# Transposing and splitting the cross-attention's context inside the self-attention stage, one batch per step

## The reference

```
x = x + self_attention(norm(x))
k = (ctx @ Wk); v = (ctx @ Wv)                  # ctx: (32, 375, 256)
x = x + softmax(norm(x) @ Wq · k / sqrt(128)) @ v @ Wo
x = x + expert(argmax(norm(x) @ wg), norm(x)) * gate
```

## Time and profile before

| | us |
|---|---|
| median of 3 runs | 2617.39 (2616.61 to 2623.79) |
| the profiled execution, its own time | 2618.37 |
| its span, first to last instruction | 2616.6 |
| PE (TensorE) busy | 2451.6 |
| PEld (its weight loads) busy | 2231.8 |
| DVE (VectorE) busy | 1759.5 |
| ACT (ScalarE) busy | 1262.5 |
| POOL (GpSimd) busy | 1050.3 |

### The profile page before, as it was taken

The page is one execution under the profiler, slowest core; times in us unless marked ns, Lnnn a source line. Parts: engine busy times, 40 slices in busy tenths (PEclk is TensorE's granted clock), DMA queues, the critical chain, the costliest instruction groups (busy, mean ns, idle before and its releaser), DMA issues. The chain is left out here.

```text
span 2616.6 us, 45419 instructions
## 1 busy us (share of the span) xinstructions
PE 2451.6 (94%) x14878; PEld 2231.8 (85%) x14878; DVE 1759.5 (67%) x4953; ACT 1262.5 (48%) x3220; POOL 1050.3 (40%) x1475
## 2 busy tenths in 40 slices
PE   5999999689999999999999989999999999999598
PEld 5888888578998989899898979999999999898476
DVE  6878887375756666565757576666757576666676
ACT  4555554364545445454545454554545454545311
POOL 3433443043434334343434343444435343434354
PEclk9999999799999999999999999999999999999799
DMA  7221223331211212122222121111111111110543
GB/s 243 73 68 57 69 67 100 110 108 53 76 64 54 68 62 77 50 72 64 72 88 62 60 69 49 58 57 38 56 56 59 48 46 56 50 35 29 185 153 122
DMA packets 98213, 195.09 MB, mean 75 GB/s; under 512 B 19696, under 2 KB 50128, under 8 KB 97728
## 3 DMA queue, kind: packets, MB, share of 16 engines
q1 hardware_dynamic: 92192, 163.68, 19.7%
q0 software_dynamic: 5600, 18.41, 2.1%
q10 hardware_dynamic: 224, 10.49, 1.2%
HBM read 127.21 MB, written 75.81 MB: 78 GB/s over the span
## 5 line engine op out<-in xcount | busy, mean ns | idle before, releaser
L1242 POOL TENSOR_SCALAR x_probs<-x_probs,x_inv 112x376 f32<-112x376 f32 x512 | 634.5, 1250 | 190.3 <-DVE x_inv L1450 190.3
L1302 ACT ACTIVATE x_probs<-x_probs,x_bias 112x376 f32<-112x376 f32 x512 | 308.4, 603 | 423.1 <-POOL x_bias L1236 423.0
L1236 POOL TENSOR_SCALAR x_bias<-x_top 112x1 f32<-112x1 f32 x512 | 124.0, 242 | 957.3 <-DVE x_top L1422 957.0
L1570 PE MATMUL x_ps_f<-x_xT,x_wq 128*128 128x448 f32 x1536 | 344.4, 374 | 12.3 <-DVE x_ctxT L1400 5.8
L1584 PE MATMUL x_ps_r<-x_wo,x_oT 128*128 128x512 f32 x1344 | 343.8, 392 | 1.4 <-DVE x_wo L1355 1.4
L1521 PEld LDWEIGHTS x_ps_o<-x_pT,x_v 128*128 128x128 f32 (+1 forms) x2304 | 294.9, 191 | 30.4 <-DVE x_pT L1429 12.7
L1570 PEld LDWEIGHTS x_ps_f<-x_xT,x_wq 128*128 128x128 f32 x1536 | 283.0, 190 | 44.0 <-DVE x_v L1400 8.8
L1521 PE MATMUL x_ps_s<-x_kT,x_qT 128*112 128x376 f32 x1536 | 312.0, 338 | 3.0 <-DVE x_top L1422 3.0
L1521 PE MATMUL x_ps_f<-x_ctxT,x_wk 128*128 128x376 f32 x1536 | 308.3, 337 | 2.5 <-DVE x_kT L1400 1.3
L1521 PE MATMUL x_ps_f<-x_wv,x_ctxT 128*128 128x512 f32 (+1 forms) x1152 | 304.6, 402 | 4.8 <-DVE x_kT L1400 4.8
L1521 PE MATMUL x_ps_o<-x_pT,x_v 128*128 128x224 f32 (+1 forms) x2304 | 298.9, 274 | 8.4 <-DVE x_pT L1429 8.4
(11 more groups left out here) (205 smaller groups left out, 3825.7 us busy)
## 6 DMA issues: line engine op xcount, KB each, us to landing
x_ctxs<-x_ctxT SPq DMA_DIRECT2D x32, 752.0 KB, 4.1
x_ctxT<-x_ctxs SPq DMA_DIRECT2D x32, 752.0 KB, 4.3
x_xT<-h2T SPq DMA_DIRECT2D x16, 896.0 KB
room<-in_ctx_dram SPq DMA_DIRECT2D x32, 256.0 KB
m_wn<-in_L_ffn_W_dram SPq DMA_DIRECT2D x32, 256.0 KB
x2r<-sums SPq DMA_DIRECT2D x28, 257.5 KB, 3.3
w_xa<-in_x_dram SPq DMA_DIRECT2D x32, 224.0 KB, 3.9
w_xr<-in_x_dram SPq DMA_DIRECT2D x32, 224.0 KB, 3.1
```

The source lines that it names most:

```text
L1236: pool.tensor_scalar(bias[:, m:m + 1], top[:, m:m + 1], -0.1 * NEG, -SCALE, ALU.max, ALU.mult) \
L1242: pool.tensor_scalar(probs[0:T, m, 0:SE], probs[0:T, m, 0:SE], inv[:, m:m + 1], None, ALU.mult).then_inc(normed, 1)
L1302: act.activation(probs[0:T, m, 0:SE], probs[0:T, m, 0:SE], ACT.Exp, bias=bias[:, m:m + 1], scale=SCALE, accum_out=total[:, m:m + 1]).then_ ...
L1570: last = pe.matmul(out[:, 0:T4], wq[:, a, c, n * D:(n + 1) * D], xT[:, b_, c, :], start=c == 0 and (a, b_) == PASSES[0], stop=c == KC - 1 ...
```

## The change

The `C` fills, the context's load and its store leave stage two and go into stage one, one batch per step. Step n handles batch (n + 2) mod 32, so that batches 0 and 1 are done last and their transposed context is still in SBUF when stage two begins. In each step:

- SP loads the next context to `room` (`load_ctx`), once TensorE has transposed the current one, and stores the previous step's result to `ctxs` (`store_ctx`), once GpSimd is done with it.
- TensorE transposes behind the scores (`context`), into the two `ps_t` banks. It waits for VectorE's low half of the previous probabilities, which frees them. The next probabilities wait until ScalarE has copied the context out.
- ScalarE copies each of the two banks twice behind the exponentials (`copy_ctx`): to `ctxT` as the high part and to `craw` (in `sums`) as it is.
- GpSimd subtracts (`low_ctx`): `craw` minus the high part is the low part.

Stage two loads all batches from 2 on with `load_ctxT`, as its second half did before.

```
 def window_attention(...):
+                def load_ctx(turn, s):
+                    n = ctx_row(turn, s)
+                    if turn.reg is None and (turn.at, s) == (0, 0):
+                        sp.wait_ge(ctx_padded, 1)
+                    else:
+                        sp.wait_ge(ctx_ready, turn.count(TB, s))
...
+                def store_ctx(turn, s):
+                    n = ctx_row(turn, s)
+                    sp.wait_ge(ctx_lo, turn.count(TB, s + 1))
...
                         load_xr(turn, s)
+                        if not (turn.reg is None and turn.at == TURNS - 1 and s == TB - 1):
+                            load_ctx(*((turn, s + 1) if s + 1 < TB else (Turn(turn.at + 1, turn.reg), 0)))
+                        if not (turn.reg is None and turn.at == 0 and s == 0):
+                            store_ctx(*back(turn, s, 1))
                         stores(turn, s, fs)
...
+                def low_ctx(turn, s):
+                    pool.wait_ge(ctx_raw, turn.count(TB, s + 1))
+                    pool.nop(nofuse=True)
+                    hi, lo = (ctxT[:, s % 2, a].rearrange("p c s -> p (c s)") for a in (HI, LO))
+                    pool.tensor_tensor(lo, craw, hi.bitcast(F32), ALU.subtract).then_inc(ctx_lo, 1)
...
                             factors2(*back(turn, s, 2))
+                        low_ctx(turn, s)
...
+                def copy_ctx(turn, s):
+                    act.wait_ge(ctx_ready, turn.count(TB, s + 1))
+                    if not (turn.reg is None and turn.at == 0 and s < 2):
+                        act.wait_ge(ctx_out[s % 2], turn.count(32, 16 * (s // 2)))
+                    for c in range(CC):
+                        act.activation(ctxT[:, s % 2, HI, c, :], ps_t[c][:, 0:SE], ACT.Copy)
+                    if not (turn.reg is None and turn.at == 0 and s == 0):
+                        act.wait_ge(ctx_lo, turn.count(TB, s))
+                    for c in range(CC):
+                        last = act.activation(craw[:, c * SE:(c + 1) * SE], ps_t[c][:, 0:SE], ACT.Copy)
+                    last.then_inc(ctx_raw, 1)
...
                         exps(turn, s)
+                        copy_ctx(turn, s)
...
+                def context(turn, s):
+                    if not (turn.reg is None and turn.at == 0 and s == 0):
+                        at, back_s = back(turn, s, 1)
+                        pe.wait_ge(pT_lo, at.count(8, 2 * back_s + 2))
+                    pe.wait_ge(ctx_in, turn.count(32 * TB, 32 * (s + 1)))
+                    for n in range(CC):
+                        for c, (k, rows) in enumerate(CHUNKS):
+                            last = pe.transpose(ps_t[n][:, k:k + rows], ctxn[0:rows, c, n * P:(n + 1) * P],
+                                                ident[0:rows, 0:rows])
+                    last.then_inc(ctx_ready, 1)
+
                 def probsT(turn, s):
+                    pe.wait_ge(ctx_raw, turn.count(TB, s + 1))
...
                         scores(turn, s)
+                        context(turn, s)
...
 def cross_attention(...):
-        if g == 2 and b + 2 < B:
-            out += [("C", b + 2, 0), ("C", b + 2, 1)]
...
-    HEAD = [("C", 0, 0), ("C", 0, 1)] + [("K", 0, g) for g in range(G)] + [("Q", 0, h) for h in range(H)] + \
-           [("C", 1, 0), ("C", 1, 1), ("V", 0, 0)]
+    HEAD = [("K", 0, g) for g in range(G)] + [("Q", 0, h) for h in range(H)] + [("V", 0, 0)]
...
-                    if B <= b + 2 < NB:
+                    if b + 2 < NB:
                         load_ctxT(b + 2)
...
-                    if b + 2 < B:
-                        keep_ctxT(b + 2)
-                    if b + 3 < B:
-                        load_ctx(b + 3)
```

More of the change, by code:

```diff
@@ L114, in free, with window_attention @@
         return self.until(turn, fill) - self.banks
-def window_attention(nc, B, T, x, Wq, bq, Wk, bk, Wv, bv, Wo, bo, x1, h2T, blanks, rest, copies):
+def window_attention(nc, B, T, x, Wq, bq, Wk, bk, Wv, bv, Wo, bo, x1, h2T, blanks, rest, copies, ctx, ctxs,
+                     ctxn, craw, ctxT):
     C = x.shape[2]
     KC = C // P
+    S, CD = ctx.shape[1:]
+    CC, SE = ctxT.shape[3:]
+    CHUNKS = [(k, min(P, SE - k)) for k in range(0, SE, P)]
+    ROT = 2
     WIN, D = 64, 32
@@ L1315, in _ @@
                     split(p)
-                for f in HEAD[10:]:
+                for f in HEAD[8:]:
                     fill(f)
@@ L1534, in fill @@
                     out = ps_f[bank_of(f)]
-                    if kind == "C":
-                        if n == 0:
-                            pe.wait_ge(ctx_in, 32 * (at + 1))
-                        for c, (k, rows) in enumerate(CHUNKS):
-                            last = pe.transpose(out[:, k:k + rows], ctxn[0:rows, c, n * P:(n + 1) * P],
-                                                ident[0:rows, 0:rows])
-                    elif kind == "R":
+                    if kind == "R":
                         pe.wait_ge(hn_ready, at + 1)
@@ L1549, in fill @@
                     elif kind == "K":
-                        half = at // B
-                        weights("k", half, n)
-                        if n == 0:
-                            if half:
-                                pe.wait_ge(ctxT_in[at % 2], 16 * ((at - B) // 2 + 1))
-                            else:
-                                pe.wait_ge(fill_done, halved(("C", at, 1)))
+                        weights("k", at // B, n)
+                        if n == 0 and at >= 2:
+                            pe.wait_ge(ctxT_in[at % 2], 16 * (at // 2))
                         last = product(out[:, 0:SE], [(wk[:, a, c, n * D:(n + 1) * D], ctxT[:, at % 2, b_, c, :])
@@ L2027, in decoder_block @@
         copies.append((own[-1], w))
-    window_attention(nc, B, T, x, attn_Wq, attn_bq, attn_Wk, attn_bk, attn_Wv, attn_bv, attn_Wo, attn_bo, x1, h2T,
-                     x2r[N:], out[N:], copies)
+    CC = ctx_1024.shape[2] // P
+    SE = S + S % 2
+    ctxs = scratch("ctxs", [B, P, 2 * CC * SE])
     with nc.sbuf_tensor("room", [P, C + N // P * E + C // P * E], F32) as room, \
             nc.sbuf_tensor("sums", [P, 2, C + 3], F32) as sums:
-        kept = [nc.alloc_semaphore(name=f"kept{n}") for n in range(2)]
-        cross_attention(nc, B, T, S, h2T, ctx_1024, mask, *own, ffn_wg, x1, x1_half, x2r, room, sums, kept)
+        with nc.sbuf_tensor("ctxT", [P, 2, 2, CC, SE], F32R) as ctxT:
+            ctxn = room[:, 0:-(-S // P) * CC * P].rearrange("p (c d) -> p c d", d=CC * P)
+            craw = sums[:].rearrange("p a c -> p (a c)")[:, 0:CC * SE]
+            window_attention(nc, B, T, x, attn_Wq, attn_bq, attn_Wk, attn_bk, attn_Wv, attn_bv, attn_Wo, attn_bo, x1, h2T,
+                             x2r[N:], out[N:], copies, ctx_1024, ctxs, ctxn, craw, ctxT)
+            kept = [nc.alloc_semaphore(name=f"kept{n}") for n in range(2)]
+            cross_attention(nc, B, T, S, h2T, ctxs, ctxT, mask, *own, ffn_wg, x1, x1_half, x2r, room, sums, kept)
         logits = room[:, C:C + N // P * E].rearrange("p (t e) -> p t e", e=E)
```

76 lines of the change are left out of this document (35 added, 41 removed).

## The result

The changed kernel takes 2613.15 us (median of 12 runs, 2604.34 to 2616.58), the kernel before 2617.6: ratio 0.9975, 95% interval 0.9963 to 0.9987. In one kernel further on (t_sp5_hib) a single run took 2752.4 us at a mean granted clock of 0.84, and its ratio leaves that run out. The profiled execution has a span of 2614.7 us, 1.9 less than before's.

A forecast was written before the change was run, and what follows sets the result against it. TensorE was taken to bound stage two, ScalarE's queue to set stage one's round. 36 + 7.3 - 15.4 - 1.5 - 4 = 22.4 us less gave 2595 us (forecast 2587 to 2603, chance 0.42; range 2578 to 2622).

The forecast's parts named there:

- The second stage: Cross attention: 64 C fills, 192 transposes, leave TensorE, saving 36 us (bounds 20 and 39).
- Its head: Start of stage two: keys start earlier (5.2 us) and batch 1's C fills go (2.1), together 7.3 us saved.
- The first turn: Stage one, 32 to 66 us: two context loads beside the weight copies cost 4 us (nothing to 17).
- rival 2: First turn stalls on its context load until the copies end at 66: 17 us instead of 4, 2608; chance 0.16.
- The turns: Stage one: ScalarE's added copies cost 2.2 us a turn, 15.4 us for seven turns.
- 56.5 to 57: Sign in the profile after: a turn in stage one takes 56.5 to 57 us.
- ScalarE's gapless queue in step 2: Stage one, step 2: from 226.5 ScalarE's queue sets the round; its copies move the next maximum by 0.7 us.
- I cost it at nothing: Stage one, step 1: TensorE's 2.1 us hold for the low half is covered by its later waits; 0 us.
- last turn: End of stage one, without N, K and Q fills: four short steps of 8 us, costing 1.5 us.
- Rival 3: Stage one: TensorE, held in order, adds to ScalarE's cost; a turn costs 7.9 us, 2635 in all; chance 0.12.
- rival 1: Stage one: ScalarE's copies are hidden, a turn costs 0.5 us; 37 us less, 2580; chance 0.2.

The follow-up runs named there:

- t_sp5_hib: Changed kernel with weight copies in six transfers, four spread over the first turn's steps, and the context's two high copies between the exponentials: 2595.3 us, 0.9913.
- t_sp5: Changed kernel with weight copies in six transfers of at most 2.1 MB, keys' and values' before the first turn, half a copy in each step: 2601.01 us, 0.9935.
- a_late: Changed kernel with the four weight copies issued behind the first turn instead of before it: 2616.77 us, 0.9988.
- a_p4: Changed kernel with the weight copies in 4 KB pieces instead of 64 KB, eight transfers instead of four: 2604.81 us, 0.9944.
- t_hib: Changed kernel with the two high copies of the context moved between the two exponentials: 2609.91 us, 0.9967.
- t_act_off: Changed kernel without ScalarE's four context copies and GpSimd's subtraction from the second turn on, TensorE's transposes kept: 2611.36 us, 0.9975.
- b_p4: The kernel before the change with its weight copies in 4 KB pieces, as a control: 2623.67 us, 1.002.

## Why the prediction was wrong, step by step

**The second stage (36 us).** Right: 33.2. **Its head (7.3).** Right: from the last bias addition to the first mask 66.6 us became 58.5, 8.1 less.

**The first turn: the step that failed.** "At half the rate 375 KB take 2.4 us [...] I take 4 us for the two." The fifth bias addition came at 129.42 us in place of 109.22, 20.2 later, where I had 6.2 (2.2 for ScalarE's copies and these 4). t_sp5, without any wait for a transfer, has it at 114.40. So the stall cost 15.0 us, or 13.7 by the second profile of the changed kernel (128.06), and the rest is 5.2: 1.8 stand before the first addition, and 1.5 are a stretch at half clock that the kernel before did not have there. Two queues do not share by rate here. In 40 to 60 us 149 pieces of the copies and 134 of the sync queue were served, and with 16-KB pieces 480 and 407: piece for piece. a_late shows that the stall (19.8 us there) goes with the copies, a_p4 that it shrinks to 3.1 with 4-KB pieces.

My rival 2 had the outcome, the load landing when the copies end, and 17 us for it; I gave it 0.16. The sum took "At half the rate", a sharing by time, and did not divide the 10.49 MB of the earlier trace rows by the 224 packets: 47 KB. Served one for one, the 375 pieces of 1 KB would let 375 times 47 KB pass, 17.6 MB, more than there is, so by this estimate the load lands only when the copies end. The Trainium skill, page "DMA: Bandwidth & Descriptors", section "Queues, rings and completion order", says that an engine goes round its queues packet by packet. The counts of this case agree with the going round; my prediction read a price near 4 out of it because it did not put the size in.

**The turns (2.2 each).** The size was near, by luck: a turn of the loop took 56.7 us on average, inside the 56.5 to 57 that I had named, for other reasons than mine. Six turns took 16.9 us more (340.2 for 323.3), where I had 13.2. At full clock it is 1.6 a turn, mostly TensorE's transposes in steps 0 and 3, not ScalarE's copies in 0 to 2. I had read ScalarE's gapless queue in step 2 as what sets the round; t_hib and t_act_off refute that (step 2 takes 8.9 us without its four copies and 9.0 with them). The other 1.2 or 1.3 a turn is the clock. "I cost it at nothing, because TensorE stands still in that step later anyway": at full clock this held, the new hold took the place of the old pause, and step 1 takes 9.9 us as before. What I had not asked is what follows a pause. With the pause ahead of the output product, the stretch at half clock behind it falls on the output product, and step 1 takes 11.2.

**Together.** First turn 14.0, turns 3.7, last turn 0.9 (2.4 for 1.5), second stage 2.8, head 0.9 the other way: 20.5 us, the difference between my 22.4 less and the 1.9 less of the two spans. Rival 3's mechanism, TensorE in order, is real, but at some 2.3 us a turn (1.0 and 1.3) of its 7.9. Of rival 1, ScalarE's copies did turn out nearly hidden (0.3 to 0.6 us a turn where it said 0.5); its time of 2580 is out, for the transposes and the stall.

**What stays open.** Why some of the pauses have a stretch at half clock behind them and others not. The two profiles of the changed kernel differ in it, so the spread of the changed kernel's runs (12 us, where the kernel before has 8) may come from there; no experiment moved the stretches alone. For the same reason it is read from the timelines, and not shown by an experiment of its own, that the moved pause is what moved the stretch. Nor was TensorE's wait ahead of the context's transposes taken out without the transposes. The changed kernel's first profile also has one such stretch in the second stage's middle that the kernel before has not, behind a pause of 1.86 us where the kernel before has one of 1.95 and no stretch: by the busy time by stretch, 0.66 of the clock from 1421 to 1426 us.

```profile
1421.00:1426.00 5.00, 5.00 (x23) 4.71 (x23) 4.05 (x16) 3.40 (x11) 2.86 (x4) 0.66 0.13 35
```

## What to carry to other kernels

Before a small transfer is put beside a bulk one, divide the bulk queue's bytes by its packets: the small one is served piece for piece, and with pieces 13 or 44 times its own on average it landed about when the bulk ended. Cut the bulk into transfers shorter than the pause between two loads, and check each of them for its own size. When an added wait takes the place of an old pause, look at what comes behind each in its engine's order: here a stretch at half clock stood behind the pause, and it moved with it.

## What the runs showed of the hardware that I had not expected

- Issuing transfers can hold the engine that issues: eight copies of 4-KB pieces held ScalarE 9.56 us at the last two (7.76 in b_p4); the same bytes in eight copies of 16-KB pieces, or in four with their rows whole, took about 0.6 us each.
- The length of a stall by piece size, the same 10.49 MB and the same load: 15.9 to 17.5 us with whole rows, 16.1 with 16 KB, 3.1 with 4 KB (there with ScalarE held besides).
- A stretch at half clock of about 3.4 us cost step 1 nothing where it fell on transposes and scores, and 1.3 us where it fell on the output product; in step 3 it cost 1.5 in both kernels. All of them in the turns stood behind pauses of TensorE of 1.9 to 2.0 us.
